# GpSimd waits for its own gathers at three places of each item instead of five

## What is computed

```python
def _gatv2(x, Wl, bl, Wr, br, att, bias, src, dst, heads, outc, concat):
    xl = (x @ Wl + bl).reshape(n, heads, outc)
    e_feat = jax.nn.leaky_relu(xl[src] + (x @ Wr + br).reshape(n, heads, outc)[dst], NEG_SLOPE)
    logits = jnp.einsum('ehc,hc->eh', e_feat, att)
    m = jax.ops.segment_max(logits, dst, num_segments=n)
    a = jnp.exp(logits - m[dst])
    denom = jax.ops.segment_sum(a, dst, num_segments=n)
    out = jax.ops.segment_sum(xl[src] * (a / denom[dst])[:, :, None], dst, num_segments=n)
    return out.reshape(n, heads * outc) + bias
# three such layers with layer norm and relu; then, with the edges' attributes:
e_aggr = segment_sum(edge_attr, dst) / max(count, 1)
h = concatenate([x, e_aggr, u[batch]]) @ W1 + b1      # batch norm, relu, @ W2, layer norm
```

## Time and profile before

| | |
|---|---|
| time, median of 3 runs | 7554.62 us (7551.28 to 7565.1) |
| profiled execution: its own time | 7553.44 us |
| profiled execution: span | 7551.0 us |
| busy: PE / weight load / DVE / ACT / POOL | 67% / 55% / 69% / 57% / 62% |
| POOL: gathers, busy, mean | 4836, 4697.6 us, 971 ns |
| mean busy share of the 16 DMA engines, software queue and hardware queue | 19.3% and 10.2% |
| mean granted TensorE clock | 0.717 |

### The profile page before, as it was taken

How to read it: one execution, slowest core, us unless ns; L and a number is a source line. 1 busy time by engine, 2 the same in 40 slices (tenths; PEclk the granted TensorE clock), 3 DMA queues, 4 the chain that set the end, 5 groups by cost and what they waited for, 6 DMA issues and landing times.

```text
span 7551.0 us, 112829 instructions
## 1 busy us (share of the span) xinstructions
PE 5087.5 (67%) x25578; PEld 4133.6 (55%) x25578; DVE 5192.5 (69%) x16259; ACT 4299.5 (57%) x10701; POOL 4698.4 (62%) x4843
## 2 busy tenths in 40 slices
PE   5778787777888656666666666655665556565556
PEld 2666666666666545555454555545544445454544
DVE  3677777777777667777777777756666666666665
ACT  2555555555555456565655565645555555555546
POOL 1666666666666566666666666656666666666640
PEclk7777777777777766667767666667777777777766
DMA  4333333333333222222222222222222222222221
GB/s 129 89 97 96 89 97 97 98 98 97 89 96 97 73 61 63 63 63 63 63 63 62 63 63 63 63 50 58 58 59 59 58 58 58 58 58 58 58 54 46
DMA packets 416504, 544.50 MB, mean 72 GB/s; under 512 B 136173, under 2 KB 325155, under 8 KB 408365
## 3 DMA queue, kind: packets, MB, share of 16 engines
q0 software_dynamic: 154752, 327.15, 19.3%
q1 hardware_dynamic: 261549, 215.52, 10.2%
HBM read 483.66 MB, written 58.58 MB: 72 GB/s over the span
## 4 chain that ended last, share of the span: by engine, by line
DMA 35%; issue 30%; POOL 29%; PE 2%; DVE 2%; POOLq 1%; ACT 1%; SPq 0%; DVEq 0%; ACTq 0%
DMA xl_g<-xl_tab,edges 34%; POOL xl_g L714 29%; PE PS L883 1%; PE PS L742 1%; PE PS L809 0%; DMA ea<-state 0%; DVE ea L1174 0%; POOLq L710 0%; PE PS L741 0%; POOLq L713 0%; ACT msg L1047 0%; DMA digit_tab<-S 0%; POOLq L712 0%; PE PS L881 0%; DVE ea L1186 0%
## 5 line engine op out<-in xcount | busy, mean ns | idle before, releaser
L714 POOL DMA_INDIRECT xl_g<-xl_tab,edges x4836 | 4697.6, 971 | 2588.7 <-issue 1409.1
L809 PE MATMUL PS<-msg,S 128*128 128x137 f32 x9672 | 1697.7, 339 | 1170.0 <-DVE msg L1334 1169.1
L809 PEld LDWEIGHTS PS<-msg,S 128*128 128x128 f32 x9672 | 1541.7, 238 | 1316.3 <-issue 794.9
L782 PE MATMUL PS<-xr_w,ST 128*128 128x132 f32 x9672 | 1922.0, 359 | 127.2 <-DVE z L1235 92.3
L1235 DVE TENSOR_TENSOR z<-PS,xl_g 128x528 f32<-128x528 f32 x1302 | 865.0, 664 | 1596.4 <-DMA xl_g<-xl_tab,edges 1317.6
L782 PEld LDWEIGHTS PS<-xr_w,ST 128*128 128x128 f32 x9672 | 1733.3, 262 | 287.2 <-issue 151.8
L967 ACT ACTIVATE distT<-PS,neg_node 128x512 f32<-128x512 f32 x1302 | 843.4, 648 | 1560.7 <-PE PS L772 1556.5
L944 ACT ACTIVATE dist<-node_row,neg_dst 128x128 f32<-128x128 f32 x4836 | 1534.5, 386 | 0.0
L1242 DVE SCALAR_TENSOR_TENSOR am<-z,att_relu 128x512 f32<-128x512 f32 x1302 | 852.1, 654 | 34.5 <-issue 17.3
L947 ACT ACTIVATE S<-dist 128x512 f32<-128x512 f32 x1302 | 780.5, 599 | 41.1
L969 ACT ACTIVATE ST<-distT 128x512 f32<-128x512 f32 x1302 | 780.2, 599 | 41.5
(11 more groups left out here) (230 smaller groups left out, 3801.0 us busy)
## 6 DMA issues: line engine op xcount, KB each, us to landing
xl_g<-xl_tab,edges POOLq DMA_INDIRECT x4836, 2.6
ea<-edge_attr SPq DMA_DIRECT2D x62, 1248.0 KB, 6.9
xr_w<-xr_tab SPq DMA_DIRECT2D x186, 66.0 KB
dst_r<-dst_rows SPq DMA_DIRECT2D x186, 64.0 KB
node_row<-node_id SPq DMA_DIRECT2D x186, 64.0 KB
state<-t_new SPq DMA_DIRECT2D x126, 68.0 KB, 1.6
st_old<-state SPq DMA_DIRECT2D x124, 68.0 KB
state<-st_new SPq DMA_DIRECT2D x124, 68.0 KB
```

Of the source, the lines that this page charges most:

```text
L714: pool.indirect_dma_start(xl_g[:, q, t, :], None, xl_tab[stage][:, :], bass.IndirectOffsetOnAxis(idx[:, q, t:t + 1], 0))\
L782: last = pe.matmul(zp[(q + g) % 2][:, n, :], ST[:, t, :], xr_w[:, q, :], start=True, stop=True)
L809: last = pe.matmul(agg_ps, S[:, q, t, :], msg[:, t, :], start=t == 0 and stage > 0, stop=t == TILES - 1)
```

## The change

One number of the table is changed.

```diff
-PACE = 5
+PACE = 8
 PAUSES = range(PACE, TILES, PACE)
 STEPS = sorted({PACE * b - 1 for b in range(1, len(PAUSES) + 1)} | {g[-1] + 1 for g in GROUPS})
 SETS = [range(a, b) for a, b in zip([0] + STEPS[:-1], STEPS)]
```

## The result

The changed kernel takes 7451.89 us (median of 4 runs, 7447.24 to 7468.18), the kernel before 7554.77 us beside it. The ratio is 0.9867, with an interval from 0.9853 to 0.9882: 1.3% faster, where the prediction had 2.9% and 7331 us, in a range from 7260 to 7430. The direction was right, but the gain was less than half of the forecast and the time lies above the range. The profiled execution took 7453.5 us, 122 us more than forecast.

The account below looks back on a forecast made before the run. GpSimd's single queue of gathers and landings was taken as the bound. From 7553.4 us, savings of 106 (stage 1), 104 (stage 2) and 12 us (stage 0) gave 7331 us, 2.9% faster, with an 8-in-10 range of 7260 to 7430.

Parts of the forecast that it names:

- What bounds the kernel: Whole kernel: GpSimd's gathers and their landings, 34% and 29% of the span, one queue waiting only for itself.
- a pause should cost ahead of gathers 8, 16 and 24 what it costs ahead of 5, 10, 15, 20 and 25: Stages 1 and 2: unchanged pause cost, 0.86 and 0.84 us over a step; two fewer save 106 and 104 us.
- They lie inside the step: GpSimd's queue: register instructions ahead of the waits come and go, but lie inside the step from gather to gather.
- The number of gathers, their bytes, all work of the other four engines ... stay as they are: All stages: gather count and bytes, other engines' work and SP's transfers unchanged; no term for longer gathers.
- two gathers stood between; I give each 0.9 us and take 13.1: Stage 0: gather 6 lands behind the load at 13.1 us into the item; net saving 12 us.
- The load keeps its place in the item, to about 0.1 us: Stage 0: the edge attributes' load is still issued some 7.15 us after the item's first gather.
- The bounds: Stage 0, gather 6's landing: at 10.06 us the stage saves 197 us, at 14.97 it is 105 us slower.
- pauses off by a tenth: Allowance in the forecast's own range, 7280 to 7400 us, beside landings of gather 6 from 12.3 to 14.
- The load doesn't hold the pause: Rival, stage 0: gather 6 gets through the load, saving 197 us instead of 12; 7146 us, chance 0.08.
- VectorE becomes the bound: Rival: VectorE's small slack is used up, half the gain of stages 1 and 2 goes; 7436 us, chance 0.08.
- Long runs slow down: Rival: gathers beyond the sixth in a run take 1.40 us, not 0.94; 684 us more, 8015 us, chance 0.05.
- Nearly no gain: Rival: removed pauses come back as longer ones, all stages save as little as stage 0; 7517 us, chance 0.03.

Follow-up runs that it names:

- at 6781 us: Changed kernel with no pause at all, each group's landings counted on its own semaphore for even and odd items: 6781.34 us, ratio 0.8946 to the kernel before.
- the second small kernel: Only gathers beside one kind of VectorE instruction per stretch; against a first such test, instruction widths now vary so that starts drift: 499.16 us.

## Why the prediction was wrong, step by step

*What bounds the kernel* was right: on every chip but the third each edit of a pause moved the time by the sum over GpSimd's own queue, down to no pause at all.

*Stages 1 and 2, "a pause should cost ahead of gathers 8, 16 and 24 what it costs ahead of 5, 10, 15, 20 and 25"*: failed by 0.08 and 0.09 us a pause. All three new places are multiples of four with a second wait; of the old five only 20 was. That is 3 x 0.085 x 62 = 16 us a stage. The pauses at 5, 17 and 25 show it. The line that waits for messages was in the prediction, as something that would never make GpSimd wait; that was right, but handling it costs time even so. "They lie inside the step" holds for the steps (0.305 us in both kernels) and not for the pauses.

*"The number of gathers, their bytes, all work of the other four engines ... stay as they are"*: true, but I took from it that a gather's length stays. It didn't: 27 ns a gather more in stage 2 (42 us), 5 in stage 1 (8 us), 9 less in stage 0 (-14 us). Shifting the gathers shifts them against lines 1242 and 1334. The term was put at nothing without a reason; that it would come out at +36 us couldn't be read from the rows, that gathers differ could. The 0.94 and 1.40 us of the earlier trace rows were both there to be seen; I put the 1.40 down to the first gather behind a pause, instead of asking what VectorE did then.

*Stage 0, "two gathers stood between; I give each 0.9 us and take 13.1"*: failed. Gather 6 lands at 14.1. Behind the load gather 8 lands 0.7 us behind gather 6 (the kernel with its pause ahead of 10 beside the changed one), not 1.8. This makes the idle time 5.11 instead of 4.2 us, 56 us. "The load keeps its place in the item, to about 0.1 us" failed too: it is issued 0.4 us earlier (6.8 us, 7.2 before). Counted from the load's issue gather 6 lands 7.3 us later, where the prediction had 6.0 (13.1 - 7.15), so the hold was mis-sized by more than the 1.0 us by which the landing was off. The bounds held it (10.06 to 14.97), and so did the note that the value lies nearer the upper end; the value taken was still too low. The pauses behind it are 0.16 us an item dearer, 10 us.

The sum of these: 56 + 10 - 14 in stage 0, 16 + 8 in stage 1, 16 + 42 in stage 2, 134 us, where the stages missed by 42, 21 and 57, 120 us. Counted over the whole trace it closes. GpSimd's idle time within the stages changed by +44, -94 and -89 us, 83 us short of the forecast -12, -106 and -104. The gathers' own time changed by +35 us where nothing was forecast, and the stretches before, between and behind the stages are 4 us longer. That is 122 us, the whole miss. So the terms for the pauses, 98 us by the means above, are 15 us too large; one reason is that a gather held right ahead of a pause shortens the pause.

*The range* allowed for the landing (12.3 to 14) and for "pauses off by a tenth", yet its upper end of 7430 was passed, since three terms were off in one direction and one of them, the gathers' length, had no place in the sum. The dearer pauses fall within the allowed tenth, by luck: their reason wasn't in the prediction.

*The rivals.* The load doesn't hold the pause: no, 6.55 us to land. VectorE becomes the bound: no, GpSimd never waits for a message in the changed kernel, and at 6781 us for 37 us in all. Long runs slow down: no, 0.94 us in runs of 18 and without end for gathers that nothing holds; gathers did get longer, but beside VectorE and not by the run. Nearly no gain: no for stages 1 and 2; for stage 0 it was what happened, and more.

## What to carry to other kernels

Where one queue sets the pace, read what else touches it: a big transfer that is issued in the same microseconds makes GpSimd idle for 5.1 us ahead of one gather where a pause elsewhere takes 1.2, and moving the pause from gather 8 to gather 5 was worth more (0.9867 to 0.9543) than the change itself. Before a wait is moved to another place, see what else the instruction there waits for. And better than fewer pauses was the question why a pause is needed: semaphores that need no order among landings gave 10.5%. And a microsecond is compared only with one from the same chip: two remainders above, of 20 and 28 us, came with the chip.

## What the runs showed of the hardware

**A gather can be starved by VectorE.** In the second small kernel, beside instructions of line 71 without a break, one gather took 16.8 us; start, us, idle before:

```profile
72.72 25.21 DVE L71 SCALAR_TENSOR_TENSOR to<-a,b 128x480 f32<-128x480 f32 x47 [0.35 <-DVE to L71]
...
77.96 1.25 POOL L50 DMA_INDIRECT got<-x,idx  x1 [0.30 <-issue]
81.94 16.82 POOL L50 DMA_INDIRECT got<-x,idx  x1 [2.73 <-issue]
99.06 0.95 POOL L50 DMA_INDIRECT got<-x,idx  x1 [0.30 <-issue]
```

It ended at 98.76, again 0.83 us behind the end of VectorE's last instruction (97.93): it was held from within one of them to the end of the thirtieth behind it.

**One chip on which the sign turned.** On the third chip the kernel before took 8581 us, and pauses at 7, 16 and 24 or at 5, 17 and 25 made it slower, ratios 1.1288 (1.1222 to 1.1353) and 1.1274 (1.1208 to 1.1339), where the fourth chip gave 0.9824 and 0.9418. With pauses at 10, 16 and 24 one execution took 10019 us there, and 7355 on the fourth. GpSimd issued at its usual pace and then stood waiting for messages, 20.5 us about once an item in stage 0. The mean granted clock of the kernel with pauses at 7, 16 and 24 was 0.65 there and 0.73 on the fourth chip, and TensorE was busy for 5481 us instead of 4908; that is far less than the 2253 us between the two times, and whether it is a cause or a result the runs don't show. Waits between the other engines ended microseconds after the work that they were for: the last product of TensorE's line 771 ahead of it ended at 5051.0 us, and ScalarE's line 966, which reads it, began at 5055.7. Less than half of the semaphore records are in that trace (59,804 against 132,739 for the same kernel on the fourth chip), so what came late can't be told, and neither can why fewer pauses made it worse. The changed kernel itself wasn't run there. On the three other chips of the experiments the kernel before took 7577 to 7583 us.
